# A fused FFN, mixer, FFN block on one core: the convolution's taps on ScalarE and their sums on GpSimd, and a routing by pair sums

## The reference

```python
x = x + 0.5 * ffn(layernorm(x))
x = x + mixer(layernorm(x))
x = x + 0.5 * ffn(layernorm(x))
```

```python
scores = sigmoid(tokens @ router_weight.T)
sfc = scores + router_bias
group_scores = top_k(sfc by group, 2).sum(-1)    # then the best 2 of 4 groups
topk_idx = top_k(sfc inside those groups, 4)
topk_w = scores at topk_idx, divided by their sum, times 2.5
```

## Time and profile before

| | |
|---|---|
| median of 3 runs | 671.64 us (671.49 to 671.74) |
| the profiled execution | 672.07 us, its span 670.3 us |
| TensorE busy, its clock | 656.8 us, granted in full (1.000) |
| VectorE busy | 548.9 us |
| GpSimd busy | 446.5 us |
| ScalarE busy | 420.7 us |

### The profile page before, as it was taken

One profiled execution on the slowest core, in us unless ns is written; L12 is line 12 of the kernel. 1 busy time (PEld: TensorE's weight loads), 2 busy tenths in 40 slices (PEclk: granted clock), 3 DMA queues, 4 the chain that ended last, 5 costly groups with the idle time before them and its releaser, 6 DMA issues. The chain is left out here.

```text
span 670.3 us, 10334 instructions
## 1 busy us (share of the span) xinstructions
PE 656.8 (98%) x3083; PEld 530.8 (79%) x3083; DVE 548.9 (82%) x1540; ACT 420.7 (63%) x804; POOL 446.5 (67%) x452
## 2 busy tenths in 40 slices
PE   8899999999999999999999999999999999999997
PEld 7787888888888887888888888888878778777675
DVE  5888889979878877879879898788979868867765
ACT  4756666675676656766476755767676566655554
POOL 2346667866776766766677775867676776776564
PEclk9999999999999999999999999999999999999999
DMA  9664909248091925629084470917419074380561
GB/s 223 144 142 99 188 11 226 51 110 162 26 224 42 215 53 124 133 80 206 17 187 101 108 147 22 227 41 168 104 32 223 2 172 100 75 181 17 118 137 32
DMA packets 60232, 78.30 MB, mean 117 GB/s; under 512 B 8176, under 2 KB 27664, under 8 KB 60176
## 3 DMA queue, kind: packets, MB, share of 16 engines
q1 hardware_dynamic: 59600, 77.63, 52.2%
q10 hardware_dynamic: 576, 0.02, 0.1%
HBM read 74.49 MB, written 3.15 MB: 116 GB/s over the span
## 5 line engine op out<-in xcount | busy, mean ns | idle before, releaser
L576 POOL TENSOR_TENSOR hid_lo<-hid,hid_hi 128x512 fp32r<-128x512 f32 x270 | 348.3, 1294 | 188.3 <-ACT hid_hi L689 188.0
L840 DVE TENSOR_TENSOR weighted<-gate_ps,raw 128x512 f32<-128x512 f32 x256 | 175.2, 684 | 69.7 <-ACT gate_ps L681 64.1
L681 ACT ACTIVATE gate_ps<-gate_ps 128x512 f32<-128x512 f32 x256 | 148.7, 581 | 119.7 <-PE gate_ps L1119 116.4
L689 ACT ACTIVATE hid_hi<-hid 128x512 fp32r<-128x512 f32 x272 | 170.4, 626 | 64.4 <-DVE hid L853 61.1
L853 DVE TENSOR_TENSOR hid<-weighted,up_ps 128x512 f32<-128x512 f32 x256 | 174.3, 681 | 8.0 <-issue 0.5
L1190 PE MATMUL down_ps<-hid_lo,wt_hi 128*128 128x512 f32 x272 | 108.0, 397 | 0.2 <-DVE hid_lo L861 0.2
L1187 PE MATMUL down_ps<-hid_hi,wt_hi 128*128 128x512 f32 x272 | 107.8, 396 | 0.0
L1188 PE MATMUL down_ps<-hid_hi,wt_lo 128*128 128x512 f32 x272 | 107.7, 396 | 0.0
L1117 PE MATMUL gate_ps<-xT_hi,wt_hi 128*128 128x512 f32 x170 | 72.0, 423 | 0.0
L1117 PE MATMUL up_ps<-xT_hi,wt_hi 128*128 128x512 f32 x170 | 68.4, 402 | 2.4 <-DVE hid L853 2.3
L1118 PE MATMUL gate_ps<-xT_lo,wt_hi 128*128 128x512 f32 x170 | 67.3, 396 | 0.0
(11 more groups left out here) (187 smaller groups left out, 1108.4 us busy)
## 6 DMA issues: line engine op xcount, KB each, us to landing
raw<-wT_hbm SPq DMA_DIRECT2D x96, 512.0 KB, 11.6
raw<-wT_hbm SPq DMA_DIRECT2D x62, 256.0 KB, 4.5
x_ln<-in_L_attn_x SPq DMA_DIRECT2D x8, 256.0 KB, 4.0
x_res<-in_L_attn_x SPq DMA_DIRECT2D x8, 256.0 KB, 3.7
out_x<-x SPq DMA_DIRECT2D x7, 256.0 KB, 2.3
raw<-in_L_ffn_gate_w SPq DMA_DIRECT2D x4, 256.0 KB, 4.9
raw<-in_L_ffn_up_w SPq DMA_DIRECT2D x4, 256.0 KB, 4.9
raw<-in_L_ffn_down_w SPq DMA_DIRECT2D x4, 256.0 KB, 5.2
```

The costliest lines, as they stand in the source:

```text
L576: nc.gpsimd.tensor_tensor(hid_lo[s][:, :], hid[s][:, :], hid_hi[s][:, :].bitcast(F32), ALU.subtract)\
L681: nc.scalar.activation(bank[:, :] if j else silu_sb[:, :], bank[:, :], ACT.Silu).then_inc(silu_done, 1)
L689: nc.scalar.activation(hid_hi[s][:, :], hid[s][:, :], ACT.Copy).then_inc(hid_hi_done, 1)
L840: V.tensor_tensor(weighted[j % 2][:, :], gate_ps[n % BANKS][:, :], wb[:, j - 1, :], ALU.mult)\
```

## The change

The four taps behind the first one become ScalarE copies with a scale (`tap`), each into a buffer of its own, and four GpSimd adds (`add tap`) sum them into `value` in SBUF. Tanh of the gate is written into `mixed` in PSUM. VectorE keeps `gate value` and `recur` (the scan). Their slots are new in all tables, and `add ln_b` moves. Routing's steps 5 to 13 become 5 to 11: sums of the pairs (i, i + 4), maxima of those pairs, the same again on the halves, and the maximum over the seven sums; `gsum` is in PSUM with a copy in SBUF, and ROUTE is 24. Steps 6 and 8 wait for nothing. `w_tok` is in the order (t, e), and its transpose, its store and the constants `spread` follow. In block 0 `silu_logits` comes one place earlier in ScalarE's list and `a_tanh` one later. The remaining routing steps are the same under new numbers.

```diff
...
-        gate_t = sb("gate_t", [P, BLK])
         val_pad = sb("val_pad", [P, SB, SEQ + 2 * PADK])
-        conv = mixed[:, :].rearrange("p (s t) -> p s t", s=SB)
+        value = sb("value", [P, BLK])
+        conv = value[:, :].rearrange("p (s t) -> p s t", s=SB)
+        tap_of = [sb(f"tap_of{n}", [P, BLK]) for n in range(4)]
...
-        best1 = sb("best1", [P, TT * NG])
-        is_best = sb("is_best", [P, TT, E])
-        others = sb("others", [P, TT, E])
-        n_best = routed[:, 388:388 + TT * NG]
-        far_single = routed[:, 404:404 + TT * NG]
-        best1_tied = sb("best1_tied", [P, TT * NG])
-        best_other = routed[:, 420:420 + TT * NG]
-        best2 = routed[:, 436:436 + TT * NG]
-        gsum = sb("gsum", [P, TT, NG])
+        HALF, QUARTER = PG // 2, PG // 4
+        PAIRS = HALF + QUARTER + 1
+        pair_sum = sb("pair_sum", [P, TT * NG, PG])
+        top_half = sb("top_half", [P, TT * NG, HALF])
+        top_quarter = sb("top_quarter", [P, TT * NG, QUARTER])
+        gsum = routed[:, 388:388 + TT * NG].rearrange("p (t g) -> p t g", t=TT)
+        gsum_too = sb("gsum_too", [P, TT, NG])
...
-        w_tok = sb("w_tok", [P, E, TT])
+        w_tok = sb("w_tok", [P, TT, E])
...
-        ROUTE = 26
+        ROUTE = 24
...
-                   "add ln_b": 16}
+                   "tap": (13, 14, 15, None), "add tap": (15, 16, None, None)}
...
-        MIXER = {"conv": (0, 0, 0, 0, 0.5, 1.5), "y high": 5, "y low": 5, "mixer out": 9, "mixer sum": 12.5,
+        MIXER = {"tap": (None, None, None, 1), "add tap": (None, None, 0, 2), "gate value": 3, "recur": 3.5,
+                 "add ln_b": 9, "y high": 5, "y low": 5, "mixer out": 9, "mixer sum": 12.5,
...
-                  "add ln_b": 16}, 0),
-                ({"conv": (15, 15.5, 16.5, 16.5, None, None)}, 0),
+                  "tap": (14, 14, 15, 16), "add tap": (15, 15, 16, None)}, 0),
...
-                ({"conv": (None, None, None, None, 0, 0), "y high": 0, "y low": 1, "mixer out": 6, "mixer sum": 6.5,
+                ({"add tap": (None, None, None, 0), "gate value": 0.5, "recur": 1, "y high": 2, "y low": 2, "add ln_b": 5,
+                  "mixer out": 6, "mixer sum": 6.5,
...
-                  "add ln_b": 16}, 1),
+                  "tap": (14, 15, 15, 16), "add tap": (15, 16, 16, None)}, 1),
...
-                ({"conv": (0, 0, 0, 0.5, 1.5, 2.5), "y high": 3, "y low": 3, "mixer out": 6, "mixer sum": 8,
-                  "stats 3": 12}, 1),
+                ({"add tap": (None, None, None, 0), "gate value": 1, "recur": 1.5, "y high": 3, "y low": 3, "add ln_b": 8,
+                  "mixer out": 6, "mixer sum": 8, "stats 3": 12}, 1),
...
-                ({"conv": (0.5, 1, 1.5, 2.5, 3.5, 4.5), "y high": 5, "y low": 4, "mixer out": 7, "mixer sum": 7.5,
+                ({"tap": (None, None, None, 1), "add tap": (None, None, 0, 2), "gate value": 3, "recur": 3.5,
+                  "y high": 5, "y low": 5, "add ln_b": 8, "mixer out": 7, "mixer sum": 7.5,
...
-                  "xT low 2": 10.5, "mixer gate": 11, "tanh gate": 13, "mixer value": 15, "copy value": 15,
-                  "add ln_b": 16}, 6),
+                  "xT low 2": 10.5, "mixer gate": 11, "tanh gate": 13, "mixer value": 14, "copy value": 14,
+                  "tap": (15, None, None, None), "add tap": (16, None, None, None)}, 6),
...
-                ({"conv": (0, 0, 0.5, 0.5, 2.5, 3.5), "y high": 5, "y low": 5, "mixer out": 7, "mixer sum": 8,
-                  "stats 3": 8.5}, 6),
+                ({"tap": (None, 0, 1, 1), "add tap": (None, 1, 2, 3), "gate value": 3.5, "recur": 4,
+                  "y high": 5, "y low": 5, "add ln_b": 8, "mixer out": 7, "mixer sum": 8, "stats 3": 8.5}, 6),
...
-                ({"stats 2": 0.5, "meanvar 2": 2, "norm 2": 0, "normalise 2": 2, "transpose 2": 9, "xT high 2": 9,
-                  "xT low 2": 8.5, "mixer gate": 10, "tanh gate": 10, "mixer value": 11, "copy value": 12,
-                  "add ln_b": 12}, 7),
-                ({"conv": (13, 13.5, 14, 14.5, 15, 15.5), "y high": 16, "y low": 16}, 7),
+                ({"stats 2": 0.5, "meanvar 2": 2, "norm 2": 0, "normalise 2": 2, "add ln_b": 5, "transpose 2": 7,
+                  "xT high 2": 7, "xT low 2": 7.5, "mixer gate": 8, "tanh gate": 8, "mixer value": 9, "copy value": 10,
+                  "tap": (11, 11, 12, 13), "add tap": (12, 12, 13, 14), "gate value": 15, "recur": 15.5,
+                  "y high": 16, "y low": 16}, 7),
...
-                sp.dma_start(wT_hbm.rearrange("e (t p) -> (e t) p", t=TT), wT[k][:, :]).then_inc(wT_stored, 16)
+                sp.dma_start(wT_hbm.rearrange("e (t p) -> t e p", t=TT), wT[k][:, :]).then_inc(wT_stored, 16)
...
+            def add_tap(b, part):
+
+                if part == 0:
+                    pool.wait_ge(first_tap_done, b + 1)
+                else:
+                    pool.wait_ge(tap_added, b * TAPS + part)
+                pool.wait_ge(tap_done, b * TAPS + part + 1)
+                nc.gpsimd.tensor_tensor(value[:, :], value[:, :], tap_of[part][:, :], ALU.add)\
+                  .then_inc(tap_added, 1)
...
-                        base=-2 * TT * q - t, pattern=[[-TT, 2], [0, I]], channel_multiplier=1))
+                        base=-E * t - 2 * q, pattern=[[-1, 2], [0, I]], channel_multiplier=1))
...
+            def tap(b, part):
+
+                act.wait_ge(mix_val_done, b + 1)
+                if b > 0:
+                    act.wait_ge(tap_added, (b - 1) * TAPS + part + 1)
+                nc.scalar.activation(tap_of[part][:, :].rearrange("p (s t) -> p s t", s=SB),
+                                     val_pad[:, :, part + 1:part + 1 + SEQ], ACT.Copy,
+                                     scale=taps_half[:, part + 1:part + 2]).then_inc(tap_done, 1)
...
-                            act.wait_ge(mix, b * MIX)
-                        nc.scalar.activation(gate_t[:, :], side[:, :], ACT.Tanh, scale=0.5)\
+                            act.wait_ge(mix, b)
+                        nc.scalar.activation(mixed[:, :], side[:, :], ACT.Tanh, scale=0.5)\
...
+                    for part, b in parts_due(steps, "tap", j):
+                        tap(b, part)
...
                 if i == 1:
+                    silu_logits(1, 0)
+                if i == 2:
                     act.wait_ge(taps_loaded, 16 * 3)
                     nc.scalar.activation(a_tanh[:, :], a_raw[:, :], ACT.Tanh).then_inc(a_done, 1)
-                if i == 2:
-                    silu_logits(1, 0)
...
+            def in_two(t):
+                return t.rearrange("p x (h c) -> p x c h", h=2)
...
-                st.wait()
+                if n not in (6, 8):
+                    st.wait()
...
                 elif n == 5:
-                    st.done(V.tensor_reduce(per_group(best1), by_group(biased), AX.X, ALU.max))
+                    st.done(V.tensor_reduce(pair_sum[:, :, 0:HALF], in_two(by_group(biased)), AX.X, ALU.add))
                 elif n == 6:
-                    st.done(V.tensor_tensor(by_group(is_best), by_group(biased), over_group(best1), ALU.is_equal))
+                    st.done(V.tensor_reduce(top_half[:, :, :], in_two(by_group(biased)), AX.X, ALU.max))
                 elif n == 7:
-                    st.done(V.scalar_tensor_tensor(others[:, :, :], is_best[:, :, :], FAR, biased[:, :, :],
-                                                   ALU.mult, ALU.add))
+                    st.done(V.tensor_reduce(pair_sum[:, :, HALF:HALF + QUARTER], in_two(top_half[:, :, :]),
+                                            AX.X, ALU.add))
                 elif n == 8:
-                    st.done(V.tensor_reduce(per_group(n_best), by_group(is_best), AX.X, ALU.add))
+                    st.done(V.tensor_reduce(top_quarter[:, :, :], in_two(top_half[:, :, :]), AX.X, ALU.max))
                 elif n == 9:
-                    st.done(V.tensor_reduce(per_group(best_other), by_group(others), AX.X, ALU.max))
+                    st.done(V.tensor_reduce(pair_sum[:, :, PAIRS - 1], top_quarter[:, :, :], AX.X, ALU.add))
                 elif n == 10:
-                    st.done(V.tensor_scalar(far_single[:, :], n_best[:, :], 1.5, FAR, ALU.is_lt, ALU.mult))
+                    st.done(V.tensor_reduce(gsum.rearrange("p t g -> p (t g)"), pair_sum[:, :, 0:PAIRS],
+                                            AX.X, ALU.max))
                 elif n == 11:
-                    st.done(V.tensor_tensor(best1_tied[:, :], far_single[:, :], best1[:, :], ALU.add))
+                    st.done(V.tensor_copy(gsum_too[:, :, :], gsum))
                 elif n == 12:
-                    st.done(V.tensor_tensor(best2[:, :], best1_tied[:, :], best_other[:, :], ALU.max))
+                    st.done(V.tensor_tensor(gdiff[:, :, :].rearrange("p t (g h) -> p t g h", g=NG),
+                                            gsum.unsqueeze(2).broadcast_to([P, TT, NG, NG]),
+                                            gsum_too[:, :, :].unsqueeze(3).broadcast_to([P, TT, NG, NG]),
```

(78 more changed lines are left out.)

15 lines of the change are left out of this document (3 added, 12 removed).

## The result

The changed kernel takes 685.96 us (685.64 to 686.16, 4 runs) against 671.6, a ratio of 1.0212 (95% interval 1.0196 to 1.0229). 676.6 was forecast with a range to 680.5: the direction was right, the size was not (14.3 us more instead of 5.0). The profiled execution took 685.85 us, its span 684.1.

What follows compares the result with a forecast made beforehand. TensorE, busy 98%, was taken as the bound, other engines counting only where it waits. Gains 3.6 and losses 8.6 made 5.0 us more: 677.1 profiled, 676.6 as median; likeliest case 673.5 to 680, with rivals 667.8 to 680.5.

Steps and rivals of the forecast that it cites:

- ScalarE's copies: Convolution taps on ScalarE: eight blocks' taps, 22 us, covered by its waits for TensorE except in the second block.
- The head: Block 0's routing: `w_tok` 2.0 us earlier, of which 1.5 count; L1235 near 18.9 instead of 20.50.
- The gains: Shorter routing and earlier silu: 1.5 in the head, 1.3 and 0.8 in the other routings, 3.6 us in all.
- the store: Store to `wT_hbm` in routing: changes order, not size, still 128 rows, costed at 0.
- The prices of a copy, of an add and of L930's successor: ScalarE tap 0.70 us, GpSimd add 1.29, the routing step that replaces L930 about 0.25.
- The arrival of the fourth add in blocks 0, 1 and 7: GpSimd's queue at the convolutions' ends: last add done at 109.0, 150.2 and 582.6.
- The loss in units 2 (without the clock's part), 3 and 13: Ends of the convolutions of blocks 0, 1 and 7: late fourth add holds `hid`, losing 2.2, 1.8 and 1.6 us.
- blocks 5 and 6: Convolutions in units 11 and 12: same insertion as blocks 2 to 4 but later, loss 0.9 each, 1.8 (0.4 to 3).
- blocks 2 to 4: Convolutions in units 5, 7 and 9: gate and scan ahead of tile 4's `hid`, loss 0.4 each, 1.2 (0 to 2.4).
- The price of a stall: Any new wait of TensorE: worth its length beyond the present slack.
- GpSimd falls further behind: Rival: adds wait for VectorE or `down` waits for `hid_lo`, 1 to 2 us more per block, 681 to 686; chance 0.08.
- the wait of `up_ps` for `hid`: Sign in the profile after: TensorE's `up_ps` waits for VectorE's `hid` 8 to 12 us instead of 2.3.

Runs made afterwards that it cites:

- E1: Kernel before with the new routing and the new place of block 0's silu of logits, convolution as before: 667.88 us, ratio 0.9946.
- E5: E1 plus 32 copies with a scale on ScalarE into buffers that nothing reads: 670.15 us, ratio 0.9979.
- E3: Changed kernel with the first three GpSimd adds of each block left out, all ScalarE copies kept: 673.17 us, ratio 1.0022.
- E9: E1 with w_tok, its transpose, its store and the constants of the spread in the old order: 666.85 us, ratio 0.9925.
- E6: Changed kernel with gate's product, scan and mixer output in later slots in unit 11 alone: 680.39 us.
- E2: Kernel before with the change's convolution and its tables alone, old routing: 687.84 us, ratio 1.0237.
- E7: E3 with unit 11's y low and value projection with its copy back in their old slots: 671.86 us.
- E12: All the changed kernel's work, w_tok in the old order, each unit in its quickest placing so far: 672.66 us, ratio 1.001.

## Why the prediction was wrong

The difference of 14.3 us, as the runs divide it: routing and silu -3.8 (E1), ScalarE's copies +2.3 (E5 less E1), the rest of the new slots and the first add +3.0 (E3 less E5), three more adds +12.8 (after less E3).

**Right.** The head: `w_tok`'s transpose at 18.83 where 18.9 was forecast. The gains, 3.8 against 3.6, but with some luck: without the new order of the store they are 4.8 (E9), and the store, costed at nothing, took 1.0 back. The prices of a copy, of an add and of L930's successor. The arrival of the fourth add in blocks 0, 1 and 7: 106.0, 152.9 and 595.2, against 109.0, 150.2 and 582.6 less or plus the shift of their units (-2.9, +2.2, +12.9), 106.1, 152.4 and 595.5. The loss in units 2 (without the clock's part), 3 and 13: 2.2, 2.2 and 1.4 against 2.2, 1.8 and 1.6. In unit 3 the size is right and the way only half: one of its two waits of 0.74 is `down` for `hid_lo`, and the other is for `weighted`, not for `hid`.

**Wrong, the step that failed.** "VectorE's queue then has `gate value` waiting for the fourth add, and behind it stand `hid`, the scan (1.21) and the next `weighted`": true for the blocks that were worked through on a time line, but blocks 5 and 6 were priced by likeness to blocks 2 to 4, at 0.9 each. In unit 11 `logit` stands there too, and with it `side`, so nearly the whole wait of 3.2 reached TensorE (3.1). E6, which meets the gate's product later, has no such wait. Block 5 cost 6.2 instead of 0.9 and is more than half of the miss of 9.4: these 3.1, the 1.6 of the clock, and waits of 0.9 and 0.7 at two moved steps; the clock and the steps are told below. Block 6 cost 1.6.

**Wrong, left out.** The price of a stall was taken to be its length. In two places the clock fell behind it, and 2.8 us in unit 2 and 1.6 in unit 11 were added (the distances of the starts in those stretches, each less the regular 0.23). The trace of before has no case of it, since its clock is 1.000; E1's own profile shows that even a wait of 0.75 can be followed by it, and E2's that the three waits of unit 2 need not be.

**Wrong, costed at nothing.** The store ("change order, not size"): 1.0. ScalarE's copies ("covered except in the second block"): 2.3. The value projection and `y low` of unit 11 one slot away: 1.3 (E7). For the first the prediction went by the bytes where the order decides; for the third it left out for whom the queue waits at the new place.

**Wrong the other way.** Blocks 2 to 4 were to lose 1.2 and lost nothing: units 5 to 10 take 238.1 against 238.3. The sums are ready there: the fourth add ends 0.2 us before the gate's product starts. The slack of `hid` falls to 0.06 in one slot of units 5, 7 and 9, so these units were near their edge too.

The rival "GpSimd falls further behind" named 681 to 686 and comes nearest in size. Its mechanism holds for a small part only. GpSimd's adds waited 0.2 us in all, but `down` did wait for `hid_lo`, 1.3 us in three places (0.36, 0.74 and 0.16). The larger part is VectorE's wait for the adds, which took more with it.

Of the signs that the prediction named, `gate value` did wait in units 2 and 3 and the gaps of units 1 to 3 add up to 3.4 us, as forecast; the wait of `up_ps` for `hid` was 4.8 instead of 8 to 12. With 3.1 at `side`, 2.1 at `gate_ps` and 1.3 at `down_ps` these waits add up to 11.3, but more than half of them came by ways that the forecast had not listed.

Open are the 2 us between E1 and E2, why some waits of 0.7 to 1.4 us are followed by the lower clock and others are not, and what the 5.8 us between E12 and E9 are made of.

## What to carry to other kernels

When a wait enters an in-order queue, list everything behind it at that place, with the buffers that each item frees, once for every irregular place: the regular ones tell nothing about them. Work taken off an engine that is not the bound gave nothing here, and work put on the others took away slack where the schedule is tight; moving the wait half a slot to a slot and a half later gave back more than half of the loss. A new order of a small transfer can change its time, even at the same bytes.

## What was not expected of the hardware

A stretch at 1.2 GHz can follow a short pause of TensorE: in E1's profile one wait of 0.75 us at 186.3, in the changed kernel waits of 0.36, 0.78 and 0.74 within 7 us. In these two kernels it lasted 3 to 7 us and cost 1.6 to 2.8. Yet waits of 0.74 and 0.74 in unit 3 and of 1.39 ahead of unit 14 of the changed kernel were not followed by one, nor were E2's waits of 0.37, 0.77 and 0.74 in unit 2. Where TensorE is the bound, a stall may cost twice its length: about 2.2 and then 2.8 in unit 2, 0.75 and then 1.7 in E1, but 3.1 and then 1.6 in unit 11.

A DMA of 64 KB took 2.5 us instead of 1.6 to its successor, with nothing changed but the order of its outer dimensions.
